# A pointwise convolution over fields without pads in 24 tiles of 1024, and a second quantisation that writes into padded rows

## What is computed

```python
def _fake_quant(x, bits):          # one scale for the whole tensor
    qmax = 2.0 ** (bits - 1) - 1.0
    scale = jnp.maximum(jnp.max(jnp.abs(x)) / qmax, 1e-08)
    y = x / scale
    yq = jnp.clip(jnp.round(y), -qmax - 1.0, qmax)   # straight-through form left out
    return yq * scale
out = jax.nn.relu(_qconv(x, w1))                     # 1x1, 32 -> 192 channels
out = jax.nn.relu(_qconv(out, w2, stride=1, padding=1, groups=PLANES))   # 3x3 depthwise, 192 channels
out = _qconv(out, w3)                                # 1x1, 192 -> 32 channels
return out + x
```

## Time and profile before

| | us |
|---|---|
| three timed runs: median (lowest, highest) | 380.57 (379.85, 380.58) |
| the profiled execution, its own time | 379.91 |
| its span in the profile | 378.1 |
| PE busy | 363.6 (96%) |
| DVE busy | 283.2 (75%) |
| ACT busy | 234.5 (62%) |
| POOL busy | 13.5 (4%) |

### The profile page before, as it was taken

The page is one execution under the profiler, slowest core; times in us unless marked ns, Lnnn a source line. Parts: engine busy times, 40 slices in busy tenths (PEclk is TensorE's granted clock), DMA queues, the critical chain, the costliest instruction groups (busy, mean ns, idle before and its releaser), DMA issues.

```text
span 378.1 us, 7791 instructions
## 1 busy us (share of the span) xinstructions
PE 363.6 (96%) x2891; PEld 268.1 (71%) x2891; DVE 283.2 (75%) x521; ACT 234.5 (62%) x380; POOL 13.5 (4%) x17
## 2 busy tenths in 40 slices
PE   8989899999999999999999999999989899999986
PEld 7768777878697879778886978797765453445533
DVE  5867678758938893697489478935986799677986
ACT  5446759545943874495459438743945997277871
POOL 6000000200030001000000000000000000000000
DMA  6947245215332612362253324134300000000005
GB/s 220 261 96 185 59 108 144 74 43 121 109 86 67 155 50 73 93 161 67 49 121 104 90 69 111 33 71 103 80 2 2 0 0 3 0 4 2 2 30 194
DMA packets 19678, 30.67 MB, mean 81 GB/s; under 512 B 4544, under 2 KB 11840, under 8 KB 19648
## 3 DMA queue, kind: packets, MB, share of 16 engines
q1 hardware_dynamic: 19008, 29.35, 29.5%
q10 hardware_dynamic: 640, 0.92, 1.1%
HBM read 10.86 MB, written 2.10 MB: 34 GB/s over the span
## 4 chain that ended last, share of the span: by engine, by line
PE 67%; DVE 13%; ACT 7%; DMA 7%; issue 4%; SPq 1%; DVEq 0%; ACTq 0%
PE sums_ps L777 22%; PE mix_ps L879 12%; PE ps L1395 9%; DMA D<-D 6%; PE mix_ps L908 5%; PE sums_ps L835 5%; PE mix_ps L883 4%; PE mix_ps L835 3%; DVE part L511 3%; PE ps L1447 3%; ACT q_I L1088 2%; ACT q_I L1090 2%; DVE part L517 2%; DVE D L502 2%; DMA x_own<-in_x_pads 1%
## 5 line engine op out<-in xcount | busy, mean ns | idle before, releaser
L777 PE MATMUL sums_ps<-D,w_hl 128*128 128x480 f32 (+1 forms) x504 | 118.2, 388 | 1.5 <-DMA D<-D 1.3
L777 PEld LDWEIGHTS sums_ps<-D,w_hl 128*128 128x128 f32 x504 | 93.2, 188 | 27.5 <-issue 5.9
L879 PE MATMUL mix_ps<-mix_hl,F_hl 128*128 128x288 f32 x360 | 64.3, 296 | 1.0 <-ACT Y L402 1.0
L402 ACT ACTIVATE Y<-mix_ps 128x288 f32<-128x288 f32 x120 | 49.0, 411 | 23.3 <-PE mix_ps L883 11.6
L879 PEld LDWEIGHTS mix_ps<-mix_hl,F_hl 128*128 128x128 f32 x360 | 55.3, 190 | 2.8 <-ACT Y L402 1.6
L340 ACT ACTIVATE r<-sums_ps,bias_sb 64x512 f32<-64x512 f32 x28 | 19.2, 684 | 42.3 <-PE sums_ps L777 42.1
L511 DVE TENSOR_TENSOR part<-mix_ps,part 64x512 f32<-64x512 f32 x16 | 11.1, 694 | 37.0 <-PE mix_ps L835 36.7
L883 PE MATMUL mix_ps<-mix_hl,X 96*128 96x288 f32 x120 | 35.3, 298 | 0.0
L1395 PE MATMUL ps<-q_q,diag 64*64 64x512 bf16 x576 | 33.4, 389 | 0.1
L360 ACT ACTIVATE D<-part 64x512 fp32r<-64x512 f32 x16 | 10.7, 669 | 32.2 <-DVE part L517 32.2
L1096 ACT ACTIVATE q_I<-ps,w_bias 128x1024 f32 x20 | 21.2, 1111 | 14.5 <-PE ps L1395 14.5
(11 more groups left out here) (143 smaller groups left out, 506.2 us busy)
## 6 DMA issues: line engine op xcount, KB each, us to landing
D<-D SPq DMA_DIRECT2D x88, 112.0 KB, 2.3
x_own<-in_x_pads SPq DMA_DIRECT2D x16, 256.0 KB, 3.3
F<-r SPq DMA_DIRECT2D x64, 64.0 KB, 2.0
F<-in_x_mix SPq DMA_DIRECT2D x16, 128.0 KB, 2.5
F<-part SPq DMA_DIRECT2D x32, 64.0 KB, 2.0
xb<-in_x_res SPq DMA_DIRECT2D x8, 256.0 KB, 2.9
out<-q_res SPq DMA_DIRECT2D x7, 256.0 KB, 2.0
w_raw<-in_w_conv SPq DMA_DIRECT2D x6, 192.0 KB, 3.9
```

Of the source, the lines that this page charges most:

```text
L402: nc.scalar.activation(Y[:, u, g], banks(p, u)[:, g % 4, 0:MIX], ACT.Copy).then_inc(y_out, 1)
L777: last = nc.tensor.matmul(tap_out(conv_sums(s, u)[:, bank, :], d), w_hl[:, wp, n, d, :], tap_in(D[f][u][:, xp], d), start=start and d == 1 ...
L879: nc.tensor.matmul(y, F_hl[u][:, xp, h, k], mix_hl[:, wp], start=n == 0, stop=False, skip_group_check=True)
```

## The change

C1 now runs over fields without pads, and the padded layout is made by the second quantisation.

1. `keep.fields` has the shape `[NP, NB, BATCH, 16, 16]`, and POOL's zeroing of it is gone. The copy from `values` (`turned_rows`) is straight for phases with `pl = 0`. For phases with `pl = 1` it is turned by one row: value rows 0 to 14 go to rows 1 to 15, and value row 15 goes to row 0. That is two instructions instead of one, so six for a pair instead of four. ACT's copies at the end become three sets of six (pair of images, third image, fourth image), one after each of `sum_done` 14, 15 and 16.
2. The first quantisation is three DVE instructions of 1024 elements and one of ACT of 1024.
3. C1 has 24 tiles of 1024 (two matmuls of 512 columns): 18 for ACT, of which 8 with bias, and 6 for DVE; 16 tiles have the offset matmuls. There are seven folds of 2048 elements after the first, then two of 1024, then 1024, 512 and 256 columns (one step more), and a reduce over 256.
4. `q2` is one run of 16 images of 17 rows of 17 with one row more (`WIDE`), column 0 of every row is a pad, and the pad at a row's right is the next row's column 0. POOL fills those columns once with 192 (546 elements a partition) after the first scale. DVE writes rows 1 to 15 of 8 images in one instruction (`inner`, 1920 elements in runs of 16 at a pitch of 17) and rows 0 and 16 of all 16 images in two (`edges`, 256 elements each), both from field row 0, multiplied by the scale or by zero depending on the partition's phase (`edge`, made from `parity`). PE's first matmul of C2 now waits for two `inner` of 480 elements and both `edges` of group 0.
5. The windows that C2 reads are shifted accordingly. The waits count the new increments. `parity` is one small reduction over `ident` in step 1.

```diff
+def turned_rows(keep, batch, m, q):
+    k = slice(32 * q, 32 * q + 32)
+    fields, values = keep.fields[k, batch, m], keep.values[k, batch, m]
+    if q % 2 == 0:
+        return [(fields, values)]
+    return [(fields[:, :, 1:PH], values[:, :, 0:PH - 1]), (fields[:, :, 0:1], values[:, :, PH - 1:PH])]
...
-            act.wait_ge(sum_done, 2 * PAIRS - 2)
-            for q in range(4):
-                nc.scalar.activation(fields_phase(keep, NB - 1, 0, q), values_phase(keep, NB - 1, 0, q), ACT.Copy)
-            act.wait_ge(sum_done, 2 * PAIRS)
...
+            for sums, m in ((2 * PAIRS - 2, slice(0, 2)), (2 * PAIRS - 1, slice(2, 3)), (2 * PAIRS, slice(3, 4))):
+                act.wait_ge(sum_done, sums)
+                for q in range(4):
+                    for fields, values in turned_rows(keep, NB - 1, m, q):
+                        last = nc.scalar.activation(fields, values, ACT.Copy)
...
                 for q in range(4):
-                    nc.vector.tensor_copy(fields_phase(keep, batch, m, q), values_phase(keep, batch, m, q))
+                    for fields, values in turned_rows(keep, batch, slice(m, m + 2), q):
+                        nc.vector.tensor_copy(fields, values)
...
+        @block.gpsimd
+        def _(pool):
+            pool.wait_ge(scale_ready, 1)
+            nc.gpsimd.memset(q2[:].rearrange("p r (n i) -> p r n i", i=FS)[:, :, :, 0], ZERO).then_inc(pads_set, 1)
...
-            for cuts in (slice(0, 2), slice(2, 6), slice(6, 9)):
-                nc.vector.tensor_scalar(x_cuts[:, cuts], f_cuts[:, cuts], sc[:, 0, 3:4], IN_BF16,
+            for b in range(NB - 1):
+                nc.vector.tensor_scalar(xq[:, b], x_fields[:, b], sc[:, 0, 3:4], IN_BF16,
                                         ALU.mult, ALU.add).then_inc(xq_ready, 1)
...
-            def quantise(g, par, batches=range(NB)):
-                for b in batches:
-                    nc.vector.tensor_scalar(q2[:, par, b], I[:, g, b, :], sc[:, 1, 3:4], ZERO,
-                                            ALU.mult, ALU.add).then_inc(q2_ready, 1)
+            def inner(g, par, images, ready):
+                nc.vector.tensor_scalar(
+                    field_rows(q2, par)[:, images, 1:PH, 1:FS], by_image(I, g)[:, images, 1:PH], sc[:, 1, 3:4], ZERO,
+                    ALU.mult, ALU.add).then_inc(ready, 1)
+            def edges(g, par, ready):
+                dve.wait_ge(edge_ready, 1)
+                for n, row in enumerate((0, PH)):
+                    nc.vector.tensor_scalar(
+                        field_rows(q2, par)[:, :, row, 1:FS], by_image(I, g)[:, :, 0], edge[:, n:n + 1], ZERO,
+                        ALU.mult, ALU.add).then_inc(ready, 1)
+            def quantise_first():
+                for b in range(2):
+                    inner(0, 0, slice(BATCH * b, BATCH * b + 2), q2_first)
+                edges(0, 0, q2_first)
+                for b in range(2):
+                    inner(0, 0, slice(BATCH * b + 2, BATCH * b + 4), q2_ready)
+                inner(0, 0, slice(BATCH * 2, BATCH * 4), q2_ready)
+            def quantise(g, par):
+                edges(g, par, q2_ready)
+                for b in range(0, NB, 2):
+                    inner(g, par, slice(BATCH * b, BATCH * (b + 2)), q2_ready)
...
-C1_TILES = 6 * NG
-C1_DVE = [3, 7, 11, 16, 20, 25, 29, 32]
+C1_TILES = NG * NB
+C1_DVE = [3, 7, 10, 13, 16, 20]
...
-C1_OFFSET = C1_DVE + [0, 1, 2, 5, 8, 10, 13, 15, 18, 21, 23, 26, 28, 31, 33, 35]
+C1_OFFSET = C1_DVE + [0, 1, 2, 5, 8, 11, 14, 17, 19, 22]
...
 def c1_slot(ps, n):
-    return ps[:, 2 * (n % 4):2 * (n % 4) + 2, 0:CUT]
+    return ps[:, 2 * (n % 4):2 * (n % 4) + 2]
...
+def field_rows(q2, par):
+    return q2[:, par, 0:IMAGES * FIELD].rearrange("p (n l i) -> p n l i", l=FS, i=FS)
+def by_image(I, g):
+    return I[:, g].rearrange("p b (m l i) -> p (b m) l i", l=PH, i=PH)
```

More of the change, by code:

```diff
@@ L52 @@
 FIELD = FS * FS
-CUT = 386
-SLOT = 3 * CUT
-assert SLOT >= BATCH * FIELD
+IMAGES = NB * BATCH
+WIDE = (IMAGES * FS + 1) * FS
 W1 = NG * NP
@@ L307, in _ @@
             nc.gpsimd.memset(keep.magic[:], IN_BF16).then_inc(keep.made, 1)
-            nc.gpsimd.memset(keep.fields[:], 0.0).then_inc(fields_zeroed, 1)
             nc.gpsimd.memset(keep.minus_zero[:], -ZERO).then_inc(keep.made, 1)
@@ L472, in _ @@
             steps(act, step)
-            act.wait_ge(sum_done, 2 * PAIRS - 2)
-            for q in range(4):
-                nc.scalar.activation(fields_phase(keep, NB - 1, 0, q), values_phase(keep, NB - 1, 0, q), ACT.Copy)
-            act.wait_ge(sum_done, 2 * PAIRS)
-            for q in range(4):
-                last = nc.scalar.activation(fields_phase(keep, NB - 1, 2, q), values_phase(keep, NB - 1, 2, q),
-                                            ACT.Copy)
+            for sums, m in ((2 * PAIRS - 2, slice(0, 2)), (2 * PAIRS - 1, slice(2, 3)), (2 * PAIRS, slice(3, 4))):
[3 more added lines that the diff above has]
+                        last = nc.scalar.activation(fields, values, ACT.Copy)
             last.then_inc(keep.last_fields, 1)
@@ L645, in sum_weights @@
                                             AX.X, ALU.add)
+                nc.vector.tensor_reduce(keep.parity[:], ident[:].rearrange("p (a b c) -> p b a c", a=2, b=2),
+                                        AX.XY, ALU.add)
                 for q in range(4):
@@ L1081, in _ @@
             act.wait_ge(scale_ready, 1)
-            nc.scalar.activation(xq[:, NB - 1, :], fields[:, NB - 1], ACT.Identity,
+            nc.scalar.activation(xq[:, NB - 1, :], x_fields[:, NB - 1], ACT.Identity,
                                  bias=keep.magic[:], scale=sc[:, 0, 3:4]).then_inc(xq_act, 1)
@@ L1205, in _ @@
+            link(nc.vector.tensor_tensor(out=c1_most[:, 0, 0:HALF // 2], in0=c1_most[:, 1, 0:HALF // 2],
+                                         in1=c1_most[:, 1, HALF // 2:HALF], op=ALU.max))
+            link(nc.vector.tensor_reduce(c1_peak[:, len(C1_DVE):], c1_most[:, 0, 0:HALF // 2], AX.X, ALU.max))
             nc.vector.tensor_reduce(stat[:, 1:2], c1_peak[:], AX.X, ALU.max).then_inc(stat_ready, 1)
             rescale(1)
-            def quantise_halves():
-                two = 2 * FIELD
-                for at, ready in ((slice(0, two), q2_first), (slice(two, SLOT), q2_ready)):
-                    for b in range(2):
-                        nc.vector.tensor_scalar(q2[:, 0, b, at], I[:, 0, b, at], sc[:, 1, 3:4], ZERO,
-                                                ALU.mult, ALU.add).then_inc(ready, 1)
@@ L1268, in fold_third @@
                 link(nc.vector.tensor_reduce(c2_peak[:, 2:3], c2_most[:, 0, 0:HALF // 2], AX.X, ALU.max))
-            quantise_halves()
-            quantise(0, 0, range(2, NB))
+            nc.vector.tensor_scalar(edge[:], keep.parity[:], sc[:, 1, 3:4], None, ALU.mult).then_inc(edge_ready, 1)
+            quantise_first()
             quantise(1, 1)
@@ L1355, in _ @@
                 for h in range(2):
-                    at = CUT * (2 * (n % 6) + h)
-                    last = nc.tensor.matmul(c1_slot(ps, n)[:, h], w_q[:, NP * (n // 6):NP * (n // 6) + NP],
-                                            x_low[:, at:at + CUT], start=n not in C1_OFFSET, stop=True,
+                    at = PX * (n % NB) + HALF * h
+                    last = nc.tensor.matmul(c1_slot(ps, n)[:, h], w_q[:, NP * (n // NB):NP * (n // NB) + NP],
+                                            x_low[:, at:at + HALF], start=n not in C1_OFFSET, stop=True,
                                             skip_group_check=True)
@@ L1378, in c2_pair @@
                 par, sets = g % 2, (g * NB + two) // 2
-                if g or two:
-                    pe.wait_ge(q2_ready, g * NB + two + 2)
-                else:
-                    pe.wait_ge(q2_first, 2)
+                if g:
+                    pe.wait_ge(q2_ready, g * 4 + (3 if two == 0 else 4) - 1)
+                elif two:
+                    pe.wait_ge(q2_ready, 3)
+                else:
+                    pe.wait_ge(pads_set, 1)
+                    pe.wait_ge(q2_first, 4)
                 if g:
@@ L1391, in c2_pair @@
                         rows = slice(64 * row, 64 * row + 64)
-                        field = q2[rows, par, two + b, 2 * h * FIELD:2 * (h + 1) * FIELD]\
-                            .rearrange("p (m l i) -> p m l i", m=2, i=FS)
+                        at = (BATCH * (two + b) + 2 * h) * FIELD + v - row + 1
+                        field = q2[rows, par, at:at + 2 * FIELD].rearrange("p (m l i) -> p m l i", m=2, i=FS)
                         at = 4 * (2 * u + v) + 2 * pi
@@ L1397, in c2_pair @@
                             diag[rows, g, at:at + 2].rearrange("p q c -> p (q c)"),
-                            field[:, :, u:u + PH, v:v + PH], start=first and row == b,
+                            field[:, :, u:u + PH, 0:PH], start=first and row == b,
                             stop=final and row != b, skip_group_check=True)
@@ L1517, in program @@
```

(1 more changed line is left out.)

43 lines of the change are left out of this document (18 added, 25 removed).

## The result

The changed kernel took 382.5 us (median of 4 executions, 381.94 to 383.21), the kernel before 380.21 beside it (4 executions, 379.61 to 380.58). The ratio is 1.006 [1.0036, 1.0084]. Twelve more executions in a later set, `after_again`, gave 382.07 for 380.67, 1.0037 [1.0013, 1.0062]. The prediction of 379.2 us and its range up to 380.9 were wrong, in the sign too. In what follows every time in a timeline counts from the start of that profile's span.

The account below looks back on a forecast made before the run. PE bounds most of the dense block and C2; ACT, PE and DVE are at their limit in C1. Dense block +0.2, C1 -2.6, tail +0.6, second quantisation +0.45 make -1.35 us: 379.2 us (378.5 to 379.9; 8 in 10 up to 380.9).

Parts of the forecast that it names:

- It costs nothing unless it gets in DVE's way.: POOL's pad memset at the first scale: 0.53 us, possibly three times that, needed by PE only 27 us later.
- rival 3: First quantisation: the memset holds up DVE by 0.56 to 1.7 us, all on the path; 380.2 us, chance 0.11.
- which moves filler matmuls only: Tail of the maximum: PE's `keep_busy` waits count one link less than there now is; no cost was given.
- the tail: Folds and reduce of the maximum after C1: 3.3 us instead of 2.71, so +0.6 us.
- from the second quantisation's start to C2: `edge`, two instructions of 480 and two of 256 before PE begins C2: 1.15 us, so +0.45 us.
- the sum for C1: DVE's 15.7 us of work plus about 1.0 of gaps, 16.75 us; first single fold at 316.45, giving -2.6 us.
- Rivals 1 and 2: Second quantisation: odd-element runs at one element a cycle (390.5 us, chance 0.08) or at half rate (379.7 us, chance 0.07).
- DVE is last, by 1.5 us: End of C1: ACT ends about 315.0 us by its sum, DVE's first single fold comes at 316.45.
- The signs named: C1: first single fold about 2.6 us earlier, ACT and PE idle now and then, DVE without gaps.
- rival 5: C1 follows ACT, not DVE, if DVE's tiles and folds are cheaper than worked: 377.9 us, chance 0.04.
- rival 4: Dense block: the copies' 0.33 us pass through in all steps, +1.8 us more, 381.0 us; chance 0.05.
- the +0.2: Dense block: two more DVE copies a step delay only step 7 through to the end, +0.2 us (0 to 0.35).

Follow-up runs that it names:

- e1_late_memset: The changed kernel with POOL's memset waiting until after DVE's three first quantisations; 380.05 us, ratio 0.9975 to the kernel before.
- e3_straight_copies: `e1_late_memset` with straight copies from values to fields for all four phases, four for a pair instead of six; 379.95 us, ratio 0.9985.
- e6_moved_copies: `e1_late_memset` with the copies from values to fields issued later in the step, behind the splits PE waits for; 380.07 us, ratio 0.9982.
- e4_half_memset: The changed kernel with the memset cut in two, one half after the first scale, the other after DVE's quantisations; 381.0 us, ratio 1.0008.
- e5_more_filler: `e1_late_memset` with more filler matmuls (`keep_busy`) on PE while DVE takes the maximum of C1; 379.4 us, ratio 0.9961.
- e7_both: `e5_more_filler` with the edit of `e6_moved_copies`; 378.7 us, ratio 0.9945.
- e2_before_memset: The kernel before with only the memset added: 546 elements at a pitch of 17 after the first scale, into an unread tile; 384.24 us, ratio 1.0101.
- f9_filler_only: The changed kernel, memset in its old place, with the added filler of `e5_more_filler`; 383.25 us, ratio 1.0054.

## Why the prediction was wrong

**The step that failed: "It costs nothing unless it gets in DVE's way."** It did get in DVE's way, and for 2.24 us. A bound was in the text (three times 0.53 at a pitch of 17, up to 1.7 us), and so was the rule; the failure is in the weight of 0.11 and in a size. No row had stood behind the factor of three. The memset takes 2.43 us, 4.6 times the row of 512, and DVE's instruction ends 0.54 us after it. The lengths tried give

| memset, us | three quantisations, us | more than without |
|---|---|---|
| 0.55 (contiguous) | 2.66 | 0.37 |
| 1.27 | 3.16 | 1.08 |
| 2.42 | 4.52 | 2.23 |
| 2.43 (the change) | 4.32 | 2.24 |

In each row the loss is the memset's length less 0.18 or 0.19 us.

The cases against rival 3 were that DVE's first instruction is ready a little earlier and that POOL may wait. It was earlier, by 0.03 us by the profile, and this helped nothing. The page of the Trainium skill was cited as the case for it and weighed as if it were a guess, because no row showed the two together. The Trainium skill's "SBUF — State Buffer" (Who interferes with whom) has a DVE instruction in a two-port mode and one of POOL take the shared ports exclusively. The trace agrees with that, with 3.00 us for an instruction of 0.74. By the same page of the Trainium skill the one that starts first gets them. The recorded starts do not show that, with DVE 0.03 us ahead and held all the same; but this is little, and spans on POOL are rough. What the hold adds, 2.24 us, is more than the whole predicted gain.

**The second: PE's `keep_busy` waits "which moves filler matmuls only".** Nothing was said of what the filler is for. The folds of 1024 and the new link make the steps between the fillers longer while each filler stays as long: PE's busy time in 318 to 322 us goes from 3.00 to 2.45 us. The clock then falls in a part of the executions. Below 0.993 are 2 of 4 and 4 of 12 of the changed kernel, 14 of 36 of `e1_late_memset`, `e3_straight_copies` and `e6_moved_copies` together and 1 of 10 of `e4_half_memset`, for none of 20 with the longer filler and the late memset, and none of 78 of the kernel before. In the profiled execution it makes +0.41 us before the second quantisation (this stretch is 2.03 us in `e5_more_filler`, 2.02 before) and +1.61 in C2. It is a loss of a part of the executions, so in a median it weighs less than that: from `e1_late_memset` to `e5_more_filler` it is 0.14%, and their intervals overlap.

**What each of the two costs** can be read from the kept profiles, because they hold the combinations. From the start of the last `mx` (the last sums) to the end of the span, which leaves the dense block out:

| profile | hold | fall before C2 | us | less the kernel before |
|---|---|---|---|---|
| `before` | no | no | 84.4 | |
| `after` | yes | yes | 86.7 | +2.3 |
| `after_again` | yes | no | 84.6 | +0.3 |
| `e1_late_memset` | no | yes | 84.1 | -0.2 |
| `e3_straight_copies`, `e5_more_filler`, `e6_moved_copies`, `e7_both` | no | no | 82.4 | -2.0 |

The hold costs 2.2 us where the clock holds, the fall 1.7 to 2.1 where it comes. Without either the change gains 2.0 us in this stretch, where the terms of the prediction gave 1.55. The hold is in both profiles of the changed kernel and turns that gain into a loss of 0.3 by itself.

**What was right.** With both out of the way, `e5_more_filler` shows the terms alone: 300.28 to 316.50 us from the first tile to the first single fold, 16.22 us (16.75 predicted); the tail 3.36 us and +0.65 (+0.6); from the second quantisation's start to C2 1.28 us and +0.57 (+0.45; `edge` lasts 0.23 us, but the next instruction starts 0.13 us after it, near the 0.1 taken, and PE begins 0.15 us after the last of `edges` has ended); C2 33.4. From the start of the first quantisation (296.60) to the first tile it has 3.68 us, +0.45, where +0.42 was worked out. Together -1.87 us, where the prediction had -1.54 for these terms. The kernel so mended is 0.39% faster by its ratio, 1.5 us, beside -1.35 in the sum. So the sum for C1 held, and the change doesn't lose by what it was about. The fit of the sum is in part luck, as the next but one paragraph shows.

**Rivals 1 and 2** fall: `inner` with 1920 elements, in runs of 16 that start in turn at an odd and an even element, takes 0.729 us, 0.72 worked out, and 1.2 or 2.2 by the rivals. The Trainium skill's "Vector Engine (DVE) Microarchitecture Reference" (5.1, Performance modes), by which the boundary makes no difference, agrees with that. The Trainium skill's "Advanced Engine Details and Errata" (VectorE Performance Modes), which asks for a start at 4 bytes, does not, and the measurement decides.

**Which engine is last in C1** was wrong for most of it: "DVE is last, by 1.5 us". The chain of waits of the changed kernel goes by PE without a break from the first tile to the last one that DVE takes, 15.2 us, and only from there by DVE:

```profile
300.07 0.62 PE ps L1378 x2
...
314.92 0.40 PE ps L1378
...
315.34 0.04 DVE q_I L1194
...
319.15 0.06 DVE q_c_most L1201
```

DVE waits 0.32 us for PE before that tile. The signs named, PE and ACT idle now and then and DVE without gaps, did not come: from 311 to 315 us PE is busy for 3.94 of 4 us, DVE for 4.00 and ACT for 3.81. The prediction had worked out 17.2 us for PE (17.0 from 300.07 to its last tile at 317.09) and weighed no rival by it. ACT's last tile ends at 319.00, 0.15 us before DVE's single fold, where 1.5 us of room was worked out. The three engines end C1 nearly together, which is why it came neither at rival 5's time nor could come much sooner. That DVE's sum gave the time so nearly is luck of this balance.

**The dense block** ended 0.96 us later in the compared profile. In step 7 the copies take 1.86 us for 1.71 and L507 starts at 269.63, 0.95 later than in the earlier trace rows, but the copies themselves start 0.91 later. So 0.04 arises there, and the rest farther ahead. Across the profiles without an early fall of the clock the last sums lie at 293.54, 294.28, 294.31 and 294.72 us with the new copies and at 293.76, 293.80, 294.22 and 294.41 with the old ones. A drift of 2 us through all steps, rival 4, is not in these; the +0.2 can be neither confirmed nor refuted. Why single executions differ by up to 1 us there stays open; in the compared pair a DMA in the chain near 151 us lasted 4.28 us for 3.81.

**Open.** In which executions of the changed kernel the clock fell, and where (before C2, or at the start of C1 as in `e2_before_memset` and `f9_filler_only`), is known for the two with a profile only. Why the same 2.45 us of PE's work lets it fall in one execution and not in another stays open too.

## What to carry to other kernels

An instruction that a change puts on an idle engine has a start time, and the profile says which instruction of another engine runs then: if that one sets the end and may be held, price the collision as the whole length of the newcomer (here it was that less 0.2 us), and price a strided memset by a row with a stride. One line of waiting put 0.6 to 0.9% right here. And where a wait of PE is bridged by filler, each link that gets longer or is added needs its filler made longer with it: read PE's busy time in the windows before and after as one of the terms of the change, and do not take one profile that kept its clock as proof that all executions do.

## What the runs showed of the hardware

- A memset of 2-byte elements on POOL at a pitch of 17 took 4.5 to 4.7 ns an element (2.43 us for 546, 1.27 for 273), contiguous 1.0 (0.55 for 546).
- A `tensor_scalar` of DVE from SBUF to SBUF that is recorded as started 0.02 to 0.03 us before POOL's memset was held by it (3.00 us for 0.74, beside a memset of 2.43); folds with two inputs and tiles from PSUM were not (1.22 us beside it and without it).
- A `tensor_scalar` over 2 elements a partition took 0.23 us, and the next instruction of DVE started 0.13 us after it.
- With PE busy for 2.45 us of four in the tail of the maximum, the clock fell behind it in two profiles of seven.
- In some executions the clock falls near 24 us. The windows of such an execution of the changed kernel, where PE waits for DMAs:

```profile
20.00:22.00 2.00, 0.81 (x4) 0.38 (x2) 1.94 (x4) 0.98 (x2) 0.00 (x0) 1.00 0.75 155
22.00:24.00 2.00, 1.12 (x5) 0.95 (x6) 0.66 (x4) 0.00 (x0) 0.00 (x0) 1.00 0.65 155
24.00:26.00 2.00, 2.00 (x7) 1.71 (x6) 0.00 (x0) 0.07 (x1) 0.00 (x0) 0.53 0.14 34
```

PE was busy for 1.93 us of the four before it. Nothing here tried to take this fall away.
